# Two attention and mixture-of-experts blocks on one core: the gate's weights multiplied into the output projection

## The reference, cut to what matters

```python
attended = attended.transpose(0, 2, 1, 3).reshape(B, L_q, D_MODEL)
attended = attended @ Wout.T + b_out
gate = jax.nn.sigmoid(attended @ Wgate.T + b_gate)
output = gate * attended + (1.0 - gate) * residual
...
x = x + _L0_xattn_ref(_layernorm(x, axis=-1), ctx_1024, ...)
x = x + _L0_ffn_ref(_layernorm(x, axis=-1), ...)
```

## Time and profile before

| what | value |
|---|---|
| median of 3 runs | 335.11 us |
| lowest and highest of the 3 | 326.82 and 341.93 us |
| span of the profiled execution, first to last instruction | 324.3 us |
| the run nearest to that span (the page gives the profiled execution no time of its own) | 326.82 us, 2.5 us above the span |
| PE, DVE, ACT, POOL busy | 77%, 48%, 36%, 42% of the span |
| share of the critical chain: PE, issue, DVE, DMA, POOL | 49%, 20%, 13%, 6%, 5% |
| mean granted TensorE clock | 0.898 of full |

### The profile page before, as it was taken

One profiled execution on the slowest core, in us unless ns is written; L12 is line 12 of the kernel. 1 busy time (PEld: TensorE's weight loads), 2 busy tenths in 40 slices (PEclk: granted clock), 3 DMA queues, 4 the chain that ended last, 5 costly groups with the idle time before them and its releaser, 6 DMA issues.

```text
span 324.3 us, 5466 instructions
## 1 busy us (share of the span) xinstructions
PE 250.7 (77%) x2044; PEld 197.2 (61%) x2044; DVE 155.1 (48%) x497; ACT 118.2 (36%) x206; POOL 137.8 (42%) x178
## 2 busy tenths in 40 slices
PE   2767999999975539999942989989987338999800
PEld 2645766667754427999941775545555328999800
DVE  3878425363775364242211964276878303332205
ACT  4033637755321023443500067965540204423200
POOL 5744602630156441355562400641267631456640
PEclk9999999999975558999995799999999959999975
DMA  7999970200011017000013920200010125001015
GB/s 241 269 224 377 219 161 2 65 3 2 0 36 34 33 33 197 16 20 26 23 36 127 361 116 0 66 1 2 0 37 33 33 82 141 15 31 36 26 29 181
DMA packets 26819, 27.02 MB, mean 83 GB/s; under 512 B 3193, under 2 KB 23844, under 8 KB 26534
## 3 DMA queue, kind: packets, MB, share of 16 engines
q1 hardware_dynamic: 23797, 21.58, 24.6%
q0 software_dynamic: 2560, 4.08, 3.9%
q10 hardware_dynamic: 432, 0.98, 0.9%
HBM read 16.76 MB, written 10.79 MB: 85 GB/s over the span
## 4 chain that ended last, share of the span: by engine, by line
PE 49%; issue 20%; DVE 13%; DMA 6%; POOL 5%; ACT 3%; another core or an unknown queue 1%; SPq 1%; POOLq 0%; DVEq 0%; ACTq 0%
PE ps L1201 8%; PE ps L1406 6%; PE ps L1178 6%; PE ps L1395 5%; PE ps L1162 4%; PE ps L1153 4%; PE ps L1133 3%; PE ps L1184 2%; DMA xres<-x 2%; DMA xe<-back 2%; DVE cst L813 2%; DMA sent<-hidk,slotu 1%; DVE attT L814 1%; PE ps L1217 1%
## 5 line engine op out<-in xcount | busy, mean ns | idle before, releaser
L559 POOL DMA_INDIRECT back<-probT,pairu x48 | 46.5, 970 | 37.4 <-DVE probT L992 15.1
L1133 PE MATMUL ps<-blank,ident 128*128 128x256 f32 x90 | 28.6, 479 | 23.6 <-DMA sent<-hidk,slotu 13.0
L1406 PE MATMUL ps<-w,hT 128*128 128x128 f32 (+1 forms) x384 | 45.0, 274 | 0.0
L804 DVE TENSOR_REDUCE peak<-ps 128x8 f32<-128x616 f32 x32 | 25.5, 798 | 40.2 <-PE ps L1153 40.2
L1406 PEld LDWEIGHTS ps<-w,hT 128*128 128x128 f32 (+1 forms) x384 | 44.2, 183 | 0.0
L654 ACT ACTIVATE probT<-ps 77x1024 f32<-77x1024 f32 x32 | 32.7, 1022 | 27.7 <-PE ps L1184 15.5
L518 POOL DMA_INDIRECT sent<-hidk,slotu x32 | 31.9, 997 | 16.4 <-issue 9.8
L1133 PEld LDWEIGHTS ps<-blank,ident 128*128 128x128 f32 x90 | 21.1, 244 | 28.5 <-issue 14.0
L531 POOL TENSOR_TENSOR w1lo<-hT,w1hi 128x1024 fp32r<-128x1024 f32 x8 | 18.9, 2366 | 40.0 <-ACT w1hi L628 40.0
L1178 PE MATMUL ps<-qst,kst 100*78 100x256 f32 x128 | 29.1, 300 | 1.0 <-ACT qst L638 1.0
L500 POOL TENSOR_SCALAR vare<-mv 128x2 f32<-128x2 f32 (+2 forms) x17 | 3.8, 226 | 52.8 <-DVE mv L786 52.3
(11 more groups left out here) (158 smaller groups left out, 474.1 us busy)
## 6 DMA issues: line engine op xcount, KB each, us to landing
sent<-blank SPq DMA_DIRECT2D x16, 193.5 KB, 8.5
xe<-sent SPq DMA_DIRECT2D x16, 193.5 KB, 4.0
back<-blank SPq DMA_DIRECT2D x16, 128.0 KB, 4.8
hT<-w1b SPq DMA_DIRECT2D x4, 512.0 KB, 6.0
w<-w2b SPq DMA_DIRECT2D x1, 2048.0 KB, 13.5
xe<-back SPq DMA_DIRECT2D x8, 256.0 KB, 3.5
hT<-w1d SPq DMA_DIRECT2D x4, 512.0 KB, 5.5
w<-w2d SPq DMA_DIRECT2D x1, 2048.0 KB, 11.4
```

Source lines behind the costliest of these rows:

```text
L559: pool.indirect_dma_start(back[m], bass.IndirectOffsetOnAxis(ap=pairu[0:n, e, c:c + 1], axis=0), ye[0:n, e, c, :], None, bounds_check=NPAI ...
L804: dve.tensor_reduce(peak[:, u % 2], s, AX.X, ALU.max, negate=True).then_inc(s_peak[a], 1)
L1133: pe.matmul(ps[:, bank, 0:GQ], ident[:], blank[:, 0:2, 0:D], start=True, stop=True)
L1406: last = pe.matmul(ps[0:n, 6 + e % 2, c * P:(c + 1) * P], hT[:, e % 2, f, c * P:c * P + n], w2[:, e, f, :], start=(f == 0), stop=(f == FC ...
```

## The change

The gate's input is y times the gate's weights plus a bias, and y is `attT` times the output weights plus a bias. The product of the two weight matrices, and of the output bias with the gate's weights, is now made once on the chip, and one matmul per tile gives y and the gate's input side by side. In detail:

- SP loads `Wout` untransposed as one more DMA of 64 KB (128 x 128 float32) into a part of `attT`, behind the router weights and ahead of the blank rows. The waits for these loads now want 80 in place of 64.
- PE at turn 4 (`GATE_TURN`) makes the product of the weights and of the output bias with the gate's weights in bank `BR` (two matmuls).
- DVE at turn 6, behind that turn's maxima, copies the product over the gate's weights and splits the summed gate bias into a high and a low row of `gater` (the first buffer of `qhi`); `gateo`, all ones, is the first buffer of `qlo`. Six instructions.
- `project` of block 0: per tile, a matmul of ones with `gater` (65 rows, 256 columns, one pass) puts the bias there, and a float32 matmul of 256 columns adds y and the gate's input.
- `gate` on PE and `projected` on ACT are gone. `tanh` on ACT reads the second half of each tile's result; `projected` on DVE reads the first and waits for `tanh`.
- The tables change; for block 0 most steps of a group stand one or two turns earlier. `next_context` on DVE goes one turn back, from 11 to 12.

```diff
-PE_STEPS = [dict(gate3=5, project=4, gate=7, turn=9, logits=10, ranks=11, next_context=8, next_parts=10,
-                 next_keys=11, turn3=7, logits3=9, ranks3=10),
+PE_STEPS = [dict(project=4, turn=8, logits=9, ranks=10, next_context=8, next_parts=10, next_keys=11,
+                 turn3=6, logits3=8, ranks3=9),
...
+        outer = attT[:, 1, P:2 * P]
+        gatef = xe[0:1, 0, 0, 0:D]
+        gater = qhi[0:LOW + 1, 0, :]
+        gateo = qlo[0:LOW + 1, 0, 0:D]
...
+            sp.dma_start(outer, wo).then_inc(s_rows, 16)
...
             def tanh(a, g):
-                act.wait_ge(s_z, g + 1)
+                act.wait_ge(s_yz, g + 1)
...
-            def projected(a, g):
-
-                act.wait_ge(s_yz, g + 1)
-                act.activation(yT, ps[:, BY, 0:GQ], ACT.Identity, bias=col[:, V_BOUT:V_BOUT + 1]).then_inc(s_yT, 1)
...
-                dve.wait_ge(s_yz, g + 1)
-                dve.wait_ge(s_yT, g + 1)
+                dve.wait_ge(s_tanh, g + 1)
...
+            def gate_weights():
+                dve.wait_ge(s_gatep, 1)
+                dve.wait_ge(s_qrep, 3)
+                dve.wait_ge(s_rows, 80)
+                dve.memset(gateo.bitcast(F32), 1.0)
+                link(dve.memset(gater.bitcast(F32), 0.0))
+                dve.tensor_copy(weight("gate0"), ps[:, BR, 0:D])
+                link(dve.tensor_tensor(gatef, ps[0:1, BR, D:2 * D], row[0:1, R_BGATE:R_BGATE + D], ALU.add))
+                link(dve.tensor_copy(gater[0:1, D:2 * D], gatef))
+                dve.tensor_tensor(gater[LOW:LOW + 1, D:2 * D], gatef, gater[0:1, D:2 * D].bitcast(F32), ALU.subtract)\
+                   .then_inc(s_gate, 1)
...
+                    if a == 0:
+                        o = ps[:, BY, k * GQ:(k + 1) * GQ]
+                        pe.matmul(o, gateo, gater, start=True, stop=False)
+                        last = pe.matmul(o, tile, both, start=False, stop=True)
...
-            def gate(a, g):
-                pe.wait_ge(s_yT, g + 1)
-                pe.wait_ge(s_yread, g + 1)
-                for k in range(GT):
-                    z = ps[:, BY, k * D:(k + 1) * D]
-                    pe.matmul(z, one[:], row[0:1, R_BGATE:R_BGATE + D], start=True, stop=False)
-                    last = pe.matmul(z, yT[:, k * P:(k + 1) * P], weight("gate0"), start=False, stop=True)
-                last.then_inc(s_z, 1)
...
+            def gate_weights():
+                pe.wait_ge(s_rows, 80)
+                pe.wait_ge(s_cst, 16)
+                pe.wait_ge(s_qstA, 3)
+                pe.wait_ge(s_qstD, 3)
+                pe.matmul(ps[:, BR, 0:D], outer, weight("gate0"), start=True, stop=True)
+                pe.matmul(ps[0:1, BR, D:2 * D], col[:, V_BOUT:V_BOUT + 1], weight("gate0"), start=True, stop=True)\
+                  .then_inc(s_gatep, 1)
```

More of the change, by code:

```diff
@@ L64 @@
 W_NAMES = ["q0", "q0p", "k0", "k0p", "v0", "out0", "gate0", "q1", "k1", "v1", "o1"]
-PE_STEPS = [dict(gate3=5, project=4, gate=7, turn=9, logits=10, ranks=11, next_context=8, next_parts=10,
-                 next_keys=11, turn3=7, logits3=9, ranks3=10),
+PE_STEPS = [dict(project=4, turn=8, logits=9, ranks=10, next_context=8, next_parts=10, next_keys=11,
+                 turn3=6, logits3=8, ranks3=9),
             dict(project=4, turn=7, logits=7, ranks=9)]
-DVE_STEPS = [dict(attended=5, projected3=6, residual3=7, hidden3=9, projected=8, residual=9, hidden=10,
-                  choose=12, slots=13, next_context=11, next_parts=13, next_keys=14, choose3=11, slots3=12),
+DVE_STEPS = [dict(attended=5, projected3=6, residual3=6, hidden3=8, projected=7, residual=7, hidden=9,
+                  choose=11, slots=12, next_context=12, next_parts=13, next_keys=14, choose3=10, slots3=11),
              dict(attended=5, residual=7, hidden=8, choose=10, slots=11)]
-ACT_STEPS = [dict(projected3=4, tanh3=5, projected=5, tanh=7, copies=8, turned=9),
+ACT_STEPS = [dict(tanh3=4, tanh=5, copies=8, turned=8),
              dict(copies=9, turned=7)]
-POOL_STEPS = [dict(deviation=10, residual=12, send=15),
+POOL_STEPS = [dict(deviation=9, residual=12, send=14),
               dict(deviation=5, residual=7, send=10)]
@@ L162, in constants, with two_block_kernel @@
     return c
-def two_block_kernel(nc, x, ctx, consts, sq, cols, rows, wg, wr, w1b, w2b, w1d, w2d, out):
+def two_block_kernel(nc, x, ctx, consts, sq, cols, rows, wg, wr, wo, w1b, w2b, w1d, w2d, out):
     F32, BF16, U32 = mybir.dt.float32, mybir.dt.bfloat16, mybir.dt.uint32
@@ L683, in weights @@
                 act.activation(wexp[:], wdif[:], ACT.Exp).then_inc(s_wexp[m], 1)
-            steps = dict(projected=projected, tanh=tanh, copies=copies, turned=turned)
+            steps = dict(tanh=tanh, copies=copies, turned=turned)
             def experts(m):
@@ L1086, in _ @@
             query_steps(0, -1)
[L1087 removed]
+            dve.wait_ge(s_rows, 80)
             link(dve.tensor_scalar(gbias[:], row[:, R_BG:R_BG + E], GATE_DIV, None, ALU.mult))
+            def gate_weights():
+                dve.wait_ge(s_gatep, 1)
+                dve.wait_ge(s_qrep, 3)
+                dve.wait_ge(s_rows, 80)
+                dve.memset(gateo.bitcast(F32), 1.0)
[5 more added lines that the diff above has]
+                   .then_inc(s_gate, 1)
             for u in range(UNITS + max(DVE_STEPS[0].values())):
                 attention(0, u)
+                if u == GATE_TURN + AHEAD:
+                    gate_weights()
                 query_steps(0, u)
@@ L1298, in next_keys @@
                     stack_k(1)
-            steps = dict(project=project, gate=gate, turn=turn, logits=logits, ranks=ranks, next_context=next_context,
+            steps = dict(project=project, turn=turn, logits=logits, ranks=ranks, next_context=next_context,
                          next_parts=next_parts, next_keys=next_keys)
+            def gate_weights():
[6 more added lines that the diff above has]
+                  .then_inc(s_gatep, 1)
             def stack_q(a, g):
@@ L1352, in attention @@
                 for u in range(UNITS + max(PE_STEPS[a].values())):
+                    if a == 0 and u == GATE_TURN:
+                        gate_weights()
                     if u < UNITS:
```

31 lines of the change are left out of this document (17 added, 14 removed).

## The result

| comparison, same chip | before, median (runs) | changed, median (lowest to highest, runs) | ratio, 95% interval |
|---|---|---|---|
| the first | 336.02 (4) | 333.3 (332.3 to 342.15, 4) | 1.017 [1.0098, 1.0242] |
| second, e1 below | 325.97 (29) | 324.92 (321.17 to 337.73, 12) | 0.9931 [0.9883, 0.9979] |
| third, e8 below | 327.48 (17) | 325.74 (320.31 to 332.45, 6) | 0.9892 [0.9813, 0.9972] |

What follows compares the result with a forecast made beforehand. Block 0's PE-full attention, then a handover chain to group 3's sends, was taken as the bound. Loop +0.4, DVE's attT 1.3 late, group 3's transposes at 104.3 against 106.28: total -2.0, 333.0 us from 335.11; range 326.5 to 338.5.

Steps and rivals of the forecast that it cites:

- The loop: PE's attention units in block 0: savings and costs sum to +0.4 us, last unit ending at 91.1 instead of 90.67.
- both gates gone: PE in block 0's attention: two of four gate matmul steps removed from the PE-bound stretch, 1.51 us each, -3.02 us.
- The stall for the held L832: Group 0's gated sum on DVE, turn 10: held by POOL's weight split, it delays the maxima and stalls PE +1.0 us.
- The logits of group 1: PE at the loop's end: they now stand ahead of the last L1201, costing about +0.5 us.
- Rival A: Group 0's gated sum on DVE: L832 isn't held, so the stall goes; -3.0 us in all, 332.0 us, chance 0.20.
- DVE behind the loop: DVE's queue up to attT of group 3: ends at 96.2 against 94.94 before, 1.3 us late.
- Rival D: PE's in-order steps wait for input under the new tables, so the change does nothing: +2.0 on forecast, 335.1 us, chance 0.13.
- The next keys: kinT and PE's projection now behind group 3's slots, some 2.3 us; fits DVE's 2.56 idle with 0.25 to spare: nothing.
- Rival C: DVE from kinT to L979: held products make the experts wait for the next keys; slower, up to 336.9 us, chance 0.10.
- The wait for the ranks: Between group 3's transposes and the sends: the unexplained 2.60 us wait stays; bounds: it stays or 1.8 goes.
- Rival B: L832 isn't held and the wait for the ranks shrinks by 1.8 us: -4.8 us, 330.3 us, chance 0.12.
- The failed step: Behind group 3's sends: experts, gathers and block 1 wait for nothing earlier, so the -2.0 us carries to the end.

Runs made afterwards that it cites:

- e1: The changed kernel again, unedited, in rounds beside the kernel before: median 324.92 us, ratio 0.9931.
- e8: The changed kernel a third time, unedited, on another chip beside the kernel before: median 325.74 us, ratio 0.9892.
- e4: The changed kernel with block 0's quarters of the experts' weights split two turns earlier (4 to 7, not 6 to 9): median 323.6 us, ratio 0.9926 to before.
- e7: The changed kernel with the copy into kinT for the next keys back at its old turn, 11 instead of 12: median 325.65 us, ratio 0.9897 to before.
- e9: The kernel of e5 run once more, on a third chip: 324.99 us, ratio 0.9823 to the kernel before.
- e5: The changed kernel with both the earlier weight split and warming multiplies ahead of the wait for the sent rows: median 322.93 us, ratio 0.9887 to before.
- e2: The changed kernel with warming multiplies (4 in block 0, 8 in block 1) ahead of PE's wait for the sent rows: median 323.22 us, ratio 0.99 to before.
- e6: The changed kernel with block 0's turns as before, except tanh3: median 332.98 us, ratio 1.0186 to the kernel before.
- e3: The kernel before with added warming multiplies ahead of PE's wait for the sent rows: median 326.25 us, ratio 1.0008 to before.
- e10: The kernel of e5 plus two warming multiplies per turn in the tail of block 0's attention: 328.82 us, ratio 0.9871 to before.

## Why the prediction was right in the stretch and wrong in the sign

**The loop.** Forecast +0.4, measured from turn 2 to the last unit's product 89.65 - 40.50 = 49.15 against 49.31, so -0.16. By terms: both gates gone as counted. `project` was over-sized: its unit takes 4.57 us (57.24 to 61.81) against 4.34, +0.23 and not +0.43; its four matmuls go by in 1.02 us from start to next start (58.47 to 59.49), where 1.30 was forecast. `gate_weights` was under-sized, 0.73 against 0.60 and inside its bounds; its six DVE instructions took 1.5 us (48.51 to 50.02; 1.6 forecast) and left 0.92 us of idle time. The stall for the held L832 was 0.86 against 1.0. The logits of group 1 took 0.54 (89.11 to 89.65) against 0.5. Rival A is dead: L832 took 1.77 us where e4 shows 0.43, and e4, in which no L536 runs beside it, gains the 1.0 us that A put on it. The Trainium skill ("SBUF — State Buffer", section "SBUF: two separate sides") has it that of a VectorE operation with two SBUF inputs and a GpSimd operation that reads SBUF the later one fully blocks. The trace agrees: L832 started 0.89 us behind the start of L536 and ended 0.28 us behind its end.

**DVE behind the loop.** `attT` of group 3 ended at 95.93 against 94.94: +1.0, where +1.3 was forecast. From there to the transposes 8.18 us, 8.1 forecast. Together 104.11 against 104.3: -2.2 for a forecast of -2.0. Rival D, which would have given the whole gain back in this stretch, has no place.

**The next keys.** DVE's idle time fell from 2.56 to 0.30 us, the figure forecast, and e7 shows that they cost nothing. Rival C fell.

**The wait for the ranks.** It stayed at 2.64 in the first profile, as assumed, but that was chance. It is 2.63 to 2.67 us in three executions (before, after, e9) and 0.64 to 1.01 in the nine others, of both kernels; e5 and e9, one kernel, have the same instructions around it to 0.02 us, and 0.87 and 2.67 us of it. Rival B's second half, that the change would remove it, has no support. What causes it stays open.

**The failed step** is in the first part: "Everything behind the sends moves with them". It doesn't: the sum had no term for what lies behind the sends, and two are needed. First, in four of five executions with the new turns and without the warming edit the experts start ahead of the clock's return, and 1.7 to 1.9 us are given back; e2 takes it away. My sum had TensorE at full clock from the experts on, because the profile of before had it so by 0.7 us. That they start sooner doesn't explain it by itself. The first warming multiply stands 4.85 us ahead of the first product in before and in after:

```profile
120.69 2.90 PE L1133 MATMUL ps<-blank,ident 128*128 128x256 f32 x6 [3.55 <-DMA sent<-hidk,slotu]
```

```profile
118.55 2.90 PE L1146 MATMUL ps<-blank,ident 128*128 128x256 f32 x6 [1.29 <-DMA sent<-hidk,slotu]
```

It does in e1, e4, e6, e7 and e8 too. Counted from it, the clock was back after 4.1 us before, 4.5 in e6 and 4.8 in e1, but after 9.1 in the changed kernel's first profile and 8.6, 8.8 and 9.0 in e4, e7 and e8. In e1, the changed kernel with its experts at 121.02:

```profile
119.00:121.00 2.00, 1.35 (x7) 0.89 (x5) 1.21 (x4) 0.00 (x0) 0.23 (x2) 0.51 0.92 249
121.00:123.00 2.00, 1.98 (x11) 1.98 (x12) 0.98 (x2) 1.09 (x3) 0.56 (x4) 1.00 1.14 306
```

What decides between the early and the late return stays open; PE's idle time ahead of the multiplies (1.29 us after, 1.21 in e1, 3.55 before) doesn't sort them. Second, from the last expert product of block 0 to block 1's attention the new turns take 40.45 to 40.87 us and the old ones, e6 among them, 40.10 to 40.12. The piece that grew lies between that product and the landing of the last rows that POOL's indirect DMAs bring back, ahead of block 1. In six executions of the new turns it is the landing, 2.95 to 3.28 us against 2.60 to 2.62 in the three of the old. The chain in e2, and then in e3:

```profile
169.68 3.16 DMA back<-probT,pairu
```

```profile
173.16 2.60 DMA back<-probT,pairu
```

In the other three (after, e9, e10) the landing is shorter than before, and the last DMA stands later behind the last expert product, 11.8 to 12.3 us against 11.0. In after:

```profile
171.99 2.11 DMA back<-probT,pairu
```

Why either happens wasn't tried; e6 shows only that it goes with the turns, not with the folded weights. So of 2.3 us the changed kernel keeps 1.8 when the experts start at full clock, and by this sum nothing when they don't.

**The size of the noise.** The sign of the first ratio needs more than these 2.3 us. The rest, the 2.3 us in block 1's attention and 2.9 at the end, differs from one execution to the next: 50.58 to 53.26 and 54.8 to 57.9 us for the same instructions of the changed kernel. The start varies too, 40.0 to 43.5 us up to turn 2. These draws are larger than the change, and that the median of 333.3 us fell on the forecast of 333.0 was luck. The prediction took 2% as what a measurement can tell. The first ratio's interval of +-0.7% excludes what the two larger comparisons found, and it can't be trusted with one execution of the kernel before in it. The two larger ones, weighted by the inverse squares of their intervals, give -0.8%, or 2.6 us; by the medians of all executions the three comparisons read -0.8, -0.3 and -0.5%. That the direct part of -2.3 us arrives in every execution is shown. That the total is faster rests on the two larger comparisons, by less than the 2% named above.

The best version is that of e5 and e9, with the earlier weight split and warming ahead of the wait: 0.9887 [0.9843, 0.9932] and 0.9823 [0.9745, 0.99] against the kernel before. That it beats the changed kernel is shown in its stretches and not in the total.

## What to carry to other kernels

Cut several executions at the same instructions and compare column by column: here a stretch that a change touches was known to 0.02 us where the total was known to 3. Ask how many executions stand on each side of a ratio before explaining its sign. When a chain is shortened, look at what the TensorE clock is doing at its end: here the work often arrived at the lower level, and a few multiplies in the wait ahead of it bought 1.8 us back, while multiplies placed inside a chain of handovers cost some 1.9 us there (e10). Removing an operation from this in-order, hand-timed schedule gained only with new turns: with the old ones the kernel was 4.8 us worse in its stretch.

## What was not expected of the hardware

The granted clock fell to about half at 240.3 us in the changed kernel's profile with PE busy 10.89 of the 12 us before, stayed there 7 us with PE busy in all of them, and did not fall there in e1. Of the last 3.25 us ahead of the fall PE was busy 2.41; the kernel before, with PE busy in 2.45 of 3.25 us at the same place (236.73 to 239.98), kept the full clock. One semaphore wait, PE's ranks to DVE, is 0.64 to 1.01 us in nine executions and 2.63 to 2.67 in three, where the profile names no instruction that ended it. The clock came back 4.1 to 4.8 us behind the first warming multiply in three executions and 8.6 to 9.1 in four. The landing of the last indirect DMA ahead of block 1 took 2.60 to 2.62 us with the old table of turns, which ends some 50 us earlier, and 2.11 to 3.28 with the new one.
